# Softmax of a cross-attention kernel: one exponential per head and tile, straight from the scores, with the maximum as bias and the sum beside it

## The reference, cut to what matters

```
logits = jnp.einsum('bqhk,bthk->bhqt', qh, kh) / scale        # scale = sqrt(128)
weights = jax.nn.softmax(logits, axis=-1)                      # over 65 keys
ctx = jnp.einsum('bhqt,bthk->bqhk', weights, vh).reshape(b, q_len, H * K)
return ctx @ wo + bo
```

## Time and profile before

| what | value |
|---|---|
| median of 3 runs | 1446.86 us (1444.49 to 1447.26) |
| the profiled execution | 1444.7 us, of which 1442.9 us are its span |
| PE busy | 1383.0 us, 96% of the span |
| DVE busy | 904.3 us, 63% |
| ACT busy | 630.3 us, 44% |
| POOL busy | 335.4 us, 23% |
| mean granted clock of PE | 0.986 of full speed |

### The profile page before, as it was taken

How to read it: one execution, slowest core, us unless ns; L and a number is a source line. 1 busy time by engine, 2 the same in 40 slices (tenths; PEclk the granted TensorE clock), 3 DMA queues, 4 the chain that set the end, 5 groups by cost and what they waited for, 6 DMA issues and landing times. The chain is left out here.

```text
span 1442.9 us, 28206 instructions
## 1 busy us (share of the span) xinstructions
PE 1383.0 (96%) x11543; PEld 1248.0 (86%) x11543; DVE 904.3 (63%) x1874; ACT 630.3 (44%) x1054; POOL 335.4 (23%) x289
## 2 busy tenths in 40 slices
PE   5999999999999999999999999997998999997898
PEld 4899999999998888899999999986887988886787
DVE  4866666666666776757666666677423587776322
ACT  4633434343343664343434343445323256665521
POOL 2201011010010212101011011015852045555654
PEclk9999999999999999999999999999999999999999
DMA  4100010000000000000000000000000000002000
GB/s 153 59 30 1 30 30 1 30 2 30 30 2 30 1 30 4 28 30 1 30 30 1 30 2 30 30 23 0 1 1 8 1 2 0 0 0 63 5 30 29
DMA packets 27994, 30.29 MB, mean 21 GB/s; under 512 B 683, under 2 KB 26867, under 8 KB 27891
## 3 DMA queue, kind: packets, MB, share of 16 engines
q1 hardware_dynamic: 27666, 28.72, 6.2%
q10 hardware_dynamic: 226, 0.10, 0.0%
HBM read 26.72 MB, written 2.10 MB: 20 GB/s over the span
## 5 line engine op out<-in xcount | busy, mean ns | idle before, releaser
L332 POOL TENSOR_TENSOR WLO<-W,WHI 128x512 fp32r<-128x512 f32 x64 | 80.8, 1292 | 765.9 <-DVE WHI L726 765.9
L167 PE MATMUL bank<-SRC_HI,WHI 128*128 128x512 f32 x576 | 230.7, 401 | 11.2 <-issue 6.9
L169 PE MATMUL bank<-SRC_HI,WLO 128*128 128x512 f32 x576 | 229.6, 399 | 0.0
L168 PE MATMUL bank<-SRC_LO,WHI 128*128 128x512 f32 x576 | 229.6, 399 | 0.0
L759 DVE STREAM_TRANSPOSE PRT<-PR 32x256 f32<-32x256 f32 x512 | 223.3, 436 | 8.4
L766 DVE TENSOR_TENSOR CLO<-bank,CHI 128x512 fp32r<-128x512 f32 x128 | 87.9, 690 | 145.6 <-ACT CHI L647 145.6
L624 ACT ACTIVATE KT<-bank,PH 128x512 f32<-128x512 f32 x128 | 88.0, 689 | 186.1 <-PE bank L169 186.1
L167 PE MATMUL bank<-WHI,CHI 128*128 128x256 f32 x576 | 167.5, 291 | 0.0
L168 PE MATMUL bank<-WLO,CHI 128*128 128x256 f32 x576 | 161.5, 280 | 0.0
L169 PE MATMUL bank<-WHI,CLO 128*128 128x256 f32 x576 | 161.0, 280 | 0.0
L167 PE MATMUL bank<-WHI,SRC_HI 128*128 128x256 f32 x512 | 148.5, 290 | 0.0
(11 more groups left out here) (189 smaller groups left out, 2878.7 us busy)
## 6 DMA issues: line engine op xcount, KB each, us to landing
W<-in_wall SPq DMA_DIRECT2D x17, 1024.0 KB, 5.5
W<-in_ctx SPq DMA_DIRECT2D x4, 512.0 KB, 7.1
X<-in_x SPq DMA_DIRECT2D x4, 512.0 KB, 8.6
mlp_w<-in_w SPq DMA_DIRECT2D x2, 1024.0 KB, 8.6
out<-X SPq DMA_DIRECT2D x4, 512.0 KB, 2.9
W<-in_wall SPq DMA_DIRECT2D x1, 512.0 KB, 7.2
W<-in_wall SPq DMA_DIRECT2D x2, 256.0 KB, 8.9
W<-in_qw SPq DMA_DIRECT2D x1, 256.0 KB, 2.8
```

The lines of the kernel that those rows point to most:

```text
L167: e.matmul(dst, a_hi, b_hi, start=start, stop=False, **kw)
L168: e.matmul(dst, a_hi, b_lo, start=False, stop=False, **kw)
L169: return e.matmul(dst, a_lo, b_hi, start=False, stop=stop, **kw)
L332: i = e.tensor_tensor(WLO[a][:, j, :, :], W[a][:, j, :, :], WHI[a][:, j, :, :].bitcast(F32), ALU.subtract)
```

## The change

The tile `sub` and its subtraction go. DVE makes, from the maximum, `nm` = -SCALE x maximum (8 columns) instead. ACT runs 8 exponentials of 65 columns, each straight from the scores in PSUM, with a column of `nm` as the bias and the sum of its row (`accum_out`) into `sm`. The sum on DVE goes. The semaphore `sub_done`, which told that the scores may be overwritten, is replaced by `exp_done`.

```diff
-            sub = sb("sub", [P, 2 * GT, KEYS], scope=ph)
+            nm = sb("nm", [P, 2 * GT], scope=ph)
@@ scores, bias_sums, and ahead of the last bias_turns (PE)
-                            e.wait_ge(sub_done, n)
+                            e.wait_ge(exp_done, n)
@@ exponential (ACT)
-                        e.wait_ge(sub_done, n + 1)
-                        e.activation(ex[:, :, :], sub[:, :, :], ACT.Exp, scale=SCALE).then_inc(exp_done, 1)
+                        e.wait_ge(nm_done, n + 1)
+                        for q in range(2 * GT):
+                            h, p = q // GT, q % GT
+                            i = e.activation(ex[:, q, :], logits[:, h, p * KEYS:(p + 1) * KEYS], ACT.Exp,
+                                             scale=SCALE, bias=nm[:, q:q + 1], accum_out=sm[:, q:q + 1])
+                        i.then_inc(exp_done, 1)
@@ softmax (DVE)
-                        e.tensor_reduce(sm[:, :], ex[:, :, :], AX_X, ALU.add).then_inc(sm_done, 1)
-                        e.wait_ge(sm_done, u + 1)
@@ shifted (DVE)
-                        e.tensor_tensor(sub[:, :, :].rearrange("p (h t) k -> p h t k", h=2), logit,
-                                        mx[:, :].rearrange("p (h t) -> p h t", h=2).unsqueeze(3)
-                                        .to_broadcast([P, 2, GT, KEYS]), ALU.subtract).then_inc(sub_done, 1)
+                        e.tensor_scalar(nm[:, :], mx[:, :], -SCALE, None, ALU.mult).then_inc(nm_done, 1)
```

More of the change, by code:

```diff
@@ L219, in program @@
             pt_out, c_hi, c_lo, kb_set = sem("pt_out"), sem("c_hi"), sem("c_lo"), sem("kb_set")
-            mx_done, sub_done, sm_done, ri_done = sem("mx_done"), sem("sub_done"), sem("sm_done"), sem("ri_done")
+            mx_done, nm_done, ri_done = sem("mx_done"), sem("nm_done"), sem("ri_done")
             p_ready, x_settled, bwt_sum = sem("p_ready"), sem("x_settled"), sem("bwt_sum")
@@ L591, in _ @@
                         up(q)
-                    e.wait_ge(sub_done, SLOTS)
+                    e.wait_ge(exp_done, SLOTS)
                     bias_turns(NL - 1, G - 1, (TB[1], None), SLOTS - 1)
```

## The result

| | before | after |
|---|---|---|
| median | 1445.74 us (6 runs, 1442.49 to 1447.26) | 1451.94 us (6 runs, 1449.86 to 1454.48) |
| the profiled execution | 1444.7 us, span 1442.9 | 1452.04 us, span 1450.3 |

The ratio is 1.0046, with a 95% interval of [1.0032, 1.0061]: slower by half a per cent, clear of noise. The forecast was 1451.5, in a range of 1447.5 to 1457.

What follows compares the result with a forecast made beforehand. PE, busy 96% of the span, bounds the kernel, so only its waits count. Five places (1.0 + 1.2 + 0.7 + 1.8 + 0.45) add 5.15 us: 1449.9 from the profile, 1452.0 from the median; taken 1451.5, range 1447.5 to 1457.

Steps and rivals of the forecast that it cites:

- The pair and the group: On ACT, an ACTIVATE and its accumulator read cost 0.30 to 0.31 us; eight pairs and a tail take 2.58 us.
- The rival with 4.0 us: Accumulator reads do not overlap, 0.50 us a pair: about +8.3 us, 1460; chance 0.08.
- Ordinary slots at 0, cover to about 3.7 us: Some 57 of 64 slots hide ACT's longer group at no cost; cover is gone beyond 3.5 us (sum 3.7).
- The rival *Faster: PE loses at least 0.13 us per ordinary slot to the softmax chain; the shorter chain returns it: 1443.8; chance 0.05.
- Slots 1, 31 and 33, margins between POOL's end and the queries: ACT's delay reaches PE's queries through POOL, less margins of 0.64, 1.26 and none: +1.2, +0.7 and +1.8 us.
- The last slot: Exponential ends later on ACT, the reciprocal on DVE follows, and the chain behind has no slack: +0.45 us.
- Slot 0: Later exponential delays the context's rounding on ACT, then DVE's softmax; PRT comes 1.0 us later and PE waits: +1.0.
- this gift of 1.45: Slot 0: PE's idle stretch splits in two; if the clock stays up, 1.45 us come back; counted as 0.
- Slot 33's clock: Behind slot 33 PE's idle time grows to 2.8 us; if the clock falls, 1.5 us are added; counted as 0.
- Slot 32 at 0: Margin of 2.09 us between POOL's end and the queries exceeds ACT's 1.94 us delay, so no cost.
- Slots 2 and 34 at 0, at most 0.4: POOL is still busy when the later chunk is ready: 0; DVE's small product may wait for POOL, 0.4 each at most.
- Busy times: ACT's busy time up by some 215 us, DVE's down by 77 us.

Runs made afterwards that it cites:

- the two lengthened kernels: Changed kernel with four of eight exponentials done twice per slot, 1469.3 us (1.0160), and with all eight done twice, 1537.9 us (1.0631).
- the chunks ahead: Changed kernel with the second scale_chunk moved ahead of the exponential in slots 1, 2 and 31 to 34: 1447.43 us, 1.0011 of before.

## Why the prediction was right, and where it was off

- **The pair and the group: right.** 0.29 us for 0.31, and 2.48 for 2.58. The rival with 4.0 us, of reads that do not overlap, falls with it.
- **Ordinary slots at 0, cover to about 3.7 us: right**, shown by 56 stretches within 0.02 us of before, and by the two lengthened kernels. The rival *Faster* falls with it. Its bound of 0.13 us a slot was that of a gain clear of noise, (5.2 + 2.9) / 64; the sign alone would have turned at 5.2 / 64 = 0.08.
- **Slots 1, 31 and 33, margins between POOL's end and the queries: right in mechanism, and close.** +1.33, +0.89 and, without the clock, +1.57, for 1.2, 0.7 and 1.8. With the chunks ahead, slots 31 and 32 were back at 0. Slot 31 cost more because the sum allowed 0.05 us from POOL's end to the product where it was 0.29. Slot 33's 1.57 lies under the 1.7 given as the least: the group was 0.1 shorter, and POOL's instruction took 1.26 for 1.54.
- **The last slot: right**, +0.38 for 0.45, and `weighted` waits for PRT there, 0.46 us.
- **Slot 0: the wait right, the sign of the stretch not.** PE's waits grew from 2.84 to 1.79 + 2.12 = 3.91, +1.07 for +1.0. (`nm` took 0.68 us there, beside POOL, for the 0.20 put; the shorter group made up for it in part.) The 3.40 us of `weighted` fell to 2.02, which gives 1.38 back. The prediction named this gift of 1.45 and left it out.
- **Slot 33's clock: named, left out, came.** +1.55 for "1.5 added". The two clock terms cancel almost wholly (-1.38 and +1.55), and that the sum survived counting both as 0 is luck. I had no reason in the trace for either: a stop as long left the clock up in two other executions.
- **Slot 32 at 0: wrong.** It cost 0.50. The failed step is the margin of 2.09 us, read from a POOL instruction of 1.31 that took 1.76 once PR lay beside it. A margin taken from one execution holds only as long as the neighbours stay where they are.
- **Slots 2 and 34 at 0, at most 0.4: mis-sized.** 0.53 each. The risk named was the right one (`nm` took 0.98 us in either slot, beside POOL), but I took half of POOL's instruction for it where it was most of it. So the second chunk came 2.1 us later against POOL's work and not 1.3, and found POOL idle. The wait with the short group cost nothing, and its removal with the long one did not bring the time back, since PR then collided.
- **Busy times: off.** ACT grew by 117.7 us and not 215: the page counts overlapping records once, and 64 groups of 2.48 less the old 41.1 are 117.6. DVE fell by 63.7 and not 77, mostly since `nm` took 0.33 us in the mean.

The sum of the stretches is 7.1 against 5.15; the 2.0 more are slots 2, 32 and 34 (1.56), 31 (0.2), and 0.2 from all the rest, in which slot 0 (-1.28) and slot 33 (+1.32) cancel. The medians differ by 6.2. The absolute forecast met so closely because the median it started from, 1446.86, later turned out to be 1.1 us high.

What stays open: which execution shows the lower clock behind a given stop. In the changed kernel a stop of 2.40 us was followed by it, in two others stops of 2.34 and 2.39 us in the same place were not, and with the sum on DVE a stop of 1.82 us was. Within one profile, with four of the exponentials doubled, a stop of 1.93 us (slot 31) was and one of 2.66 us (slot 34) was not. So the length of the stop alone does not decide. Each kernel was profiled once, so how often each happens isn't known.

## What to carry to other kernels

When work moves to an engine, walk its queue and ask at each step what stands behind the lengthened instruction: here 56 slots hid 1.84 us more without loss, and the eight others paid all of the 6 to 7 us (slot 0 in its wait, which the clock gave back). Swapping the lines in the queue, so that what the next stage waits for goes ahead, brought it back (1445.27 against 1445.59), but the same order also helped the kernel before, which stayed ahead by 2.6 us. An accidental wait may keep two engines off each other; measure again after it is removed.

## What the runs showed of the hardware

- An ACTIVATE of 65 columns from PSUM with a bias column and a collected sum takes 0.29 us from one to the next, of which the collecting is 0.09. Without it eight took 1.76 us, (1.76 - 0.33) / 7 = 0.20 from one to the next.
- A DVE product over only 8 columns took 0.17 us in the median and up to 0.98 beside POOL, with its source in SBUF; with the source in PSUM it took 0.166 to 0.168 in all 64 slots, POOL busy or not.
- Two `tensor_tensor` instructions of 512 columns on POOL took 2.56 us back to back, and 2.99 to 3.05 with DVE's PR (two sources in SBUF) getting in between.
- TensorE's granted clock fell after a stop of 1.82 us in one kernel and did not after 2.34 and 2.39 us in two others, at the same place; in one profile it fell after 1.93 and not after 2.66 us. Where one stop of 2.84 us had become two of 1.79 and 2.12 with work between, `weighted` ran at full speed, 1.38 us shorter.
- PE's products of 512 columns start 0.23 us apart while each record lasts 0.39, so a short wait costs more than its length: 0.26 us of waiting made 0.50.
